# Attention's weighed sums of two steps stand together, with three buffers of probabilities and one of stacked operands; GpSimd in one loop over the routed tiles

## The reference, cut to what matters

```python
x = x + xattn(layernorm(x), ctx)      # 32 heads of 16; q and k are rms-normed per head
x = x + ffn(layernorm(x))             # one shared expert and 7 routed ones, top 2 of 7

def xattn(x, ctx):
    q, k, v = x @ Wq.T, ctx @ Wk.T, ctx @ Wv.T       # k and v interleaved by features
    scores = rmsnorm(q) @ rmsnorm(k).T * 16 ** -0.5
    return softmax(scores) @ v

def ffn(x):
    gate = x @ Wr + br
    _, ids = top_k(gate + gate_bias, 2)              # probs: softmax over the two chosen gates
    u = x @ Wup + bup                                # each expert
    g = silu(u @ Wgate + bgate) * u
    return sum_e(probs_e * (g @ Wdown + bdown)) + shared_expert(x)
```

## Time and profile before

| what | value |
|---|---|
| median of 3 runs | 972.75 us (972.32 to 972.9) |
| profiled execution | 973.43 us |
| its span (first to last instruction) | 971.7 us |
| mean granted clock of PE, share of full | 0.996 |
| busy: PE | 946.0 us (97%) |
| busy: PEld | 682.0 us (70%) |
| busy: DVE | 707.2 us (73%) |
| busy: ACT | 497.8 us (51%) |
| busy: POOL | 208.4 us (21%) |

### The profile page before, as it was taken

One profiled execution on the slowest core, in us unless ns is written; L12 is line 12 of the kernel. 1 busy time (PEld: TensorE's weight loads), 2 busy tenths in 40 slices (PEclk: granted clock), 3 DMA queues, 4 the chain that ended last, 5 costly groups with the idle time before them and its releaser, 6 DMA issues.

```text
span 971.7 us, 17895 instructions
## 1 busy us (share of the span) xinstructions
PE 946.0 (97%) x6676; PEld 682.0 (70%) x6676; DVE 707.2 (73%) x1459; ACT 497.8 (51%) x619; POOL 208.4 (21%) x226
## 2 busy tenths in 40 slices
PE   8999999999999999999999999899999999999995
PEld 6634444454434543446999889799999999999995
DVE  7798767886678767885978787665867686858654
ACT  4588668866787658887324223322424243424221
POOL 1011000311012200321300001333233333233331
PEclk9999999999999999999999999999999999999998
DMA  9400100101101110324413114633544536635533
GB/s 330 169 1 23 65 1 1 45 33 39 61 1 44 45 66 1 110 75 163 176 44 112 65 56 144 204 65 54 178 80 123 131 77 193 187 66 157 117 56 41
DMA packets 32512, 87.42 MB, mean 90 GB/s; under 512 B 7744, under 2 KB 7744, under 8 KB 28352
## 3 DMA queue, kind: packets, MB, share of 16 engines
q1 hardware_dynamic: 21920, 60.70, 17.8%
q0 software_dynamic: 10528, 25.87, 13.1%
HBM read 61.83 MB, written 24.72 MB: 89 GB/s over the span
## 4 chain that ended last, share of the span: by engine, by line
PE 83%; DVE 7%; DMA 4%; issue 3%; ACT 2%; POOLq 1%; DVEq 0%; POOL 0%; SPq 0%; ACTq 0%
PE z_ps L905 15%; PE y_ps L905 14%; PE u_ps L905 13%; PE o_ps L640 11%; PE scores L624 8%; PE bank_a L677 5%; PE bank_b L661 5%; PE bank_b L647 2%; PE xt_ps L917 2%; PE bank_a L647 2%; DMA out<-y_sb,target 2%; PE tr L706 1%; PE tr L700 1%; PE tr L695 1%; DMA xg<-xn_dram,index 1%
## 5 line engine op out<-in xcount | busy, mean ns | idle before, releaser
L1178 ACT ACTIVATE probs<-scores 128x2048 f32<-128x2048 f32 x128 | 240.7, 1880 | 64.1 <-PE scores L624 61.1
L905 PE MATMUL z_ps<-u_hi,w_sb 128*128 128x256 f32 x896 | 168.3, 285 | 0.7 <-DVE u_lo L1867 0.7
L905 PE MATMUL u_ps<-x_hi,w_sb 128*128 128x256 f32 x864 | 159.2, 282 | 0.0
L1208 ACT ACTIVATE u_hi<-u_ps,b_ug 128x256 fp32r<-128x256 f32 x108 | 45.4, 471 | 197.6 <-PE u_ps L905 176.3
L905 PEld LDWEIGHTS z_ps<-u_hi,w_sb 128*128 128x128 f32 x896 | 141.0, 190 | 2.1 <-DVE u_lo L1867 1.2
L905 PE MATMUL y_ps<-w_sb,g_hi 128*128 128x512 f32 x448 | 139.5, 392 | 0.2 <-DVE g_lo L1885 0.2
L905 PEld LDWEIGHTS u_ps<-x_hi,w_sb 128*128 128x128 f32 x864 | 135.7, 190 | 1.1
L640 PE MATMUL o_ps<-probs,v_sb 128*17 128x512 f32 x1024 | 134.7, 598 | 0.0
L905 PE MATMUL z_ps<-u_lo,w_sb 128*128 128x256 f32 x448 | 126.6, 282 | 0.0
L905 PE MATMUL u_ps<-x_lo,w_sb 128*128 128x256 f32 x432 | 122.0, 282 | 0.0
L1220 ACT ACTIVATE s_sb<-z_ps,b_ug 128x256 f32<-128x256 f32 x112 | 47.0, 472 | 103.4 <-PE z_ps L905 103.4
(11 more groups left out here) (248 smaller groups left out, 1596.3 us busy)
## 6 DMA issues: line engine op xcount, KB each, us to landing
w_raw<-w_all SPq DMA_DIRECT2D x27, 1024.0 KB, 7.7
ctx_raw<-ctx_t SPq DMA_DIRECT2D x4, 1024.0 KB, 6.8
out<-x_sb SPq DMA_DIRECT2D x16, 256.0 KB, 2.0
xg<-xt_dram POOLq DMA_DIRECT2D x14, 256.0 KB
x_sb<-x SPq DMA_DIRECT2D x1, 3072.0 KB, 17.2
xn<-x_t SPq DMA_DIRECT2D x12, 256.0 KB, 4.7
xn_dram<-xn SPq DMA_DIRECT2D x12, 256.0 KB, 2.1
xt_dram<-xt SPq DMA_DIRECT2D x6, 512.0 KB, 3.0
```

The lines of the kernel that those rows point to most:

```text
L905: ins = nc.tensor.matmul(out_ps, stat[a], mov[b], start=(first and a + b == 0), stop=(last and a == 1), skip_group_check=True)
L1178: nc.scalar.activation(probs[:, t % 2], scores[:], ACT.Exp).then_inc(p_ready, 1)
L1208: last = nc.scalar.activation(u_hi[:, c, :], u_ps[:, b, a, :], ACT.Identity, bias=b_ug[:, par, 0, c:c + 1])
```

## The change

In the attention: a step's `weighed` calls are given by a table, `SUMMED`, which says for each `s` which steps' sums stand in it. Pairs stand in steps 0, 3 and 6, single ones in 2 and 4, none in 1, 5 and 7. In steps 2 and 7 `between` comes ahead of them, in the others behind them. The turns are dealt out anew, few in the steps with a pair. The probabilities have three buffers, and ACT waits for `weighed(t-3)`. The stacked operands have one buffer; DVE waits in `half_scored` until the unit before has read its half. `sum_q` of step 7 comes ahead of the turns.

In the FFN: `table_part` moves from behind the up stage to behind the gate stage, and writes into `xt_ps`; `table_out` moves from ahead of `x_low` to the time of the down stage. GpSimd has a single loop, and waits for a scatter's landing at the start of the next scatter, behind the next gather.

```diff
-        probs = asb("probs", [P, 2, QUADS, SEQ])
+        probs = asb("probs", [P, 3, QUADS, SEQ])
...
-        q_st = asb("q_st", [P, 2, 2, SEQ], FP32R)
-        k_hi, k_lo = (asb(n, [P, 2, 2, CTX], FP32R) for n in ("k_hi", "k_lo"))
+        q_st = asb("q_st", [P, 2, SEQ], FP32R)
+        k_hi, k_lo = (asb(n, [P, 2, CTX], FP32R) for n in ("k_hi", "k_lo"))
...
-        K_TURNS = {6: (0, 4), 7: (4, 5), 0: (5, 9), 1: (9, 12)}
-        Q_TURNS = {3: (0, 5), 4: (5, 9), 5: (9, 12)}
+        K_TURNS = {6: (0, 1), 7: (1, 5), 0: (5, 6), 1: (6, 12)}
+        Q_TURNS = {3: (0, 1), 4: (1, 6), 5: (6, 12)}
+
+        SUMMED = {0: (-2, -1), 1: (), 2: (0,), 3: (1, 2), 4: (3,), 5: (), 6: (4, 5), 7: ()}
...
             def gather(n):
 
-                if isinstance(n, int):
+                first = isinstance(n, int) and n == NA
+                if first:
                     pool.wait_ge(xl_done, n * 2)
-                else:
-                    pool.wait_ge(xt_ready, (n - NT) * 2)
-                if isinstance(n, int):
                     pool.wait_ge(table_ready, 1)
                     pool.wait_ge(dense_stored, 16)
                 else:
+                    pool.wait_ge(xt_ready, (n - NT) * 2)
                     pool.wait_ge(row_saved, n - NA)
...
-            def scatter(n, more=True):
-
+
+            def scatter(n):
+                if not isinstance(n, int):
+                    pool.wait_ge(y_stored, (n - NA + 1) * 32)
+                    pool.sem_inc(passed)
...
-                if more:
-                    pool.wait_ge(y_stored, (n - NA + 2) * 32)
-                    pool.sem_inc(passed)
...
-            def turn(n, par, j):
-                gather(n + 1)
-                pool.wait_ge(out_stored, 16 * TILES)
-                scatter(n - 1)
-
-            total = routed(pool, lambda j, par, nth, first: None, turn)
-            scatter(total + NA - 1, more=False)
+
+            pool.wait_ge(start_ready, 1)
+            total = bound(pool, ER)
+            gather(NA + 1)
+            pool.wait_ge(out_stored, 16 * TILES)
+            scatter(NA - 1)
+            with pool.Fori(1, total) as i:
+                gather(i + (NA + 1))
+                scatter(i + (NA - 1))
+            scatter(total + (NA - 1))
...
                 elif s == 7:
                     if ahead:
+                        sum_q(u + 2)
                         k_turns(u + 2, *K_TURNS[s])
-                    if ahead:
-                        sum_q(u + 2)
...
             for u in range(UNITS):
                 for s in range(STEPS):
+
                     scored(u, s)
-                    between(u, s)
-                    if u or s:
-                        weighed(STEPS * u + s - 1)
+                    if s in (2, 7):
+                        between(u, s)
+                    for back in SUMMED[s]:
+                        if u or back >= 0:
+                            weighed(STEPS * u + back)
+                    if s not in (2, 7):
+                        between(u, s)
                     after(u, s)
             first_up(5 * UP_TURNS, len(UPS))
             pe.wait_ge(p_ready, STEPS * UNITS)
-            weighed(STEPS * UNITS - 1)
+            for t in (STEPS * UNITS - 2, STEPS * UNITS - 1):
+                weighed(t)
...
             def x_transposes(n):
                 if isinstance(n, int) and n < NT:
                     return
+                if isinstance(n, int):
+                    pe.wait_ge(window_read, 3)
...
-            def table_part(n, w):
+            def table_part(w):
 
                 pe.wait_ge(hots_ready, w + 1)
-                pe.wait_ge(y_done, 2 * n)
-                at = y_v[:, 0, 0:COLS]
+                pe.wait_ge(window_read, w + 1)
+                at = xt_ps[:, 0].rearrange("p a n -> p (a n)")[:, 0:COLS]
...
-            tile(5, 0, behind_up=lambda: table_part(5, 0), windows=2, bounds=range(1, DC + 1))
-            tile(6, 0, behind_up=lambda: table_part(6, 1), windows=3, bounds=range(DC + 1, ER + 1))
+            tile(5, 0, behind_z=lambda: table_part(0), bounds=range(1, DC + 1))
+            tile(6, 0, behind_z=lambda: table_part(1), bounds=range(DC + 1, ER + 1))
...
-                    if t > 1:
-                        act.wait_ge(pv_done, t - 1)
+                    if t > 2:
+                        act.wait_ge(pv_done, t - 2)
...
-                    nc.scalar.activation(probs[:, t % 2], scores[:], ACT.Exp).then_inc(p_ready, 1)
+                    nc.scalar.activation(probs[:, t % 3], scores[:], ACT.Exp).then_inc(p_ready, 1)
...
+            def half_scored(u, ab):
+                if u:
+                    dve.wait_ge(sc_ready, STEPS * (u - 1) + MT * (ab + 1))
...
-            tile(5, 0, x_tile=10, during_u=lambda: hot_cols(0), before_x=lambda: table_out(0),
-                 during_y=lambda: hot_rows(1))
+            tile(5, 0, x_tile=10, during_u=lambda: hot_cols(0),
+                 during_y=steps_of(lambda: table_out(0), lambda: hot_rows(1)))
...
-            tile(6, 0, x_tile=12, during_u=lambda: hot_cols(1), before_x=lambda: table_out(1),
-                 during_y=splits(1, 1, [1]))
+            tile(6, 0, x_tile=12, during_u=lambda: hot_cols(1),
+                 during_y=steps_of(lambda: table_out(1), splits(1, 1, [1])))
```

More of the change, by code:

```diff
@@ L623, in scored @@
                         rows = slice(32 * j, 32 * j + 32)
-                        last = nc.tensor.matmul(scores[:, j, :], part[rows, u % 2, ab, mt * P:(mt + 1) * P],
-                                                q_st[rows, u % 2, ab, :], start=(part is k_hi), stop=(part is k_lo),
+                        last = nc.tensor.matmul(scores[:, j, :], part[rows, ab, mt * P:(mt + 1) * P],
+                                                q_st[rows, ab, :], start=(part is k_hi), stop=(part is k_lo),
                                                 skip_group_check=True)
@@ L640, in weighed @@
                     last = nc.tensor.matmul(o_ps[32 * j:32 * j + HD + 1, :], v_sb[b % 2][:, mt, head, :],
-                                            probs[:, t % 2, j, :], start=(mt == 0), stop=(mt == MT - 1),
+                                            probs[:, t % 3, j, :], start=(mt == 0), stop=(mt == MT - 1),
                                             skip_group_check=True)
@@ L944, in table_part, with tile @@
                 last.then_inc(window_ready, 1)
-            def tile(n, par, j=0, behind_up=None, amid_z=None, behind_z=None, windows=0, bounds=()):
+            def tile(n, par, j=0, behind_up=None, amid_z=None, behind_z=None, bounds=()):
                 w = w_sb[par]
@@ L985, in tile @@
                     behind_z()
-                if windows:
-                    pe.wait_ge(window_read, windows)
-                elif known and n == 2:
+                if known and n == 2:
                     pe.wait_ge(gates_read, 1)
@@ L1425, in stack_q @@
                 done(nc.vector.stream_shuffle(twin[:], qn[:], (UPPER_TWICE, LOWER_TWICE)[ab]))
-                at = q_st[:, u % 2, ab, :]
+                at = q_st[:, ab, :]
+                half_scored(u, ab)
                 done(nc.vector.tensor_copy(at, twin[:]))
@@ L1433, in stack_k @@
                 done(nc.vector.stream_shuffle(twin[:], kn[:], (UPPER_TWICE, LOWER_TWICE)[ab]))
-                hi = k_hi[:, u % 2, ab, :]
+                hi = k_hi[:, ab, :]
+                half_scored(u, ab)
                 done(nc.vector.tensor_scalar(hi, twin[:], sign[:, 0:1], None, ALU.mult))
-                nc.vector.scalar_tensor_tensor(k_lo[:, u % 2, ab, :], twin[:], sign[:, 0:1], hi.bitcast(FP32),
+                nc.vector.scalar_tensor_tensor(k_lo[:, ab, :], twin[:], sign[:, 0:1], hi.bitcast(FP32),
                                                ALU.mult, ALU.subtract).then_inc(k_stacked, 1)
@@ L1845, in table_out @@
                 dve.wait_ge(window_ready, w + 2)
-                part = y_v[:, 0, 0:COLS]
+                part = xt_ps[:, 0].rearrange("p a n -> p (a n)")[:, 0:COLS]
                 if w == 0:
```

## The result

The changed kernel takes 966.92 us (median; 966.54 to 968.92). Its ratio to the kernel before is 0.9947 [0.9932, 0.9961]: faster by 0.53%, or 5.8 us, where 12.2 were forecast. Its profiled execution is one at the median, 966.92, with a span of 965.1.

What follows compares the result with a forecast made beforehand. PE, busy for 97% of the span at almost full clock, was taken as the bound. Attention -4.2 and FFN -8.0 make -12.2 us, from 972.75 to 960.5; range for 8 in 10: 956.5 to 966.5.

Steps and rivals of the forecast that it cites:

- Step 2: unchanged, 2.72: Attention, regular units: step 2 was to keep its length of 2.72 us.
- Steps 5 and 7 ... 2.72 each: Attention, regular units: PE work of 2.70 and 2.66 us, so 2.72 each by the exponential.
- The pair: Attention, steps 0, 3, 6: two adjacent weighed sums take 1.845 us, saving 0.115 a pair.
- a second sum saves nothing: Rival for the attention's pairs: weight loads don't overlap on the same rows; price 5.5 us, total 966.0; chance 0.12.
- Unit 0, -0.7: Attention, unit 0: three turns move from step 0 into step 1, where PE waits for the exponential; -0.7 us.
- Units 14 and 15, +2.6: Last two attention units: no turns to even out the pairs, so about 23.6 and 22.8 us; +2.6 us.
- The new waits, no cost: Attention: the third probabilities buffer and DVE's wait for the unit before cost nothing; tightest margin 2.3 us.
- The table, -2.1: FFN tiles 5 and 6: PE's stand of 1.05 us for DVE's one-hot columns goes; two tiles, -2.1 us.
- The first gather, "margin 1.8 us": FFN: index at 575.6, packets end at 581.3, transposes need them at 583.1; margin 1.8 us despite the later table.
- second rival: GpSimd part does less: tile 10's gather still late, or the first misses its 1.8 us; 962.5 to 966; chance 0.10.
- Tile 9's gather, -4.2, and the clock behind it, -1.35: FFN: PE's 4.15 us wait for gathered rows goes, -4.2; so does the clock's fall behind it, -1.35 us.
- The rival of the clock in units 14 and 15: Attention's last units: PE's clock falls in steps with little work, giving about 980 us; chance 0.04.

Runs made afterwards that it cites:

- e5: Changed kernel with step 1's output transposes between turns 9 and 10 instead of behind all six turns; 965.87 us.
- e6: Changed kernel, but from unit 14's step 1 on each step has one weighed sum, behind `between`, as before the change; 964.16 us.
- e8: Changed kernel with step 7's four turns ahead of `sum_q` instead of behind it; 973.72 us.
- e9: Changed kernel with the waits for the next unit's stacked operands ahead of step 7's last turn instead of the next scores; 966.19 us.
- e10: Changed kernel with `between` in the middle of pairs of weighed sums instead of behind them; 973.25 us.
- e4: Kernel before with only the new buffer counts and DVE's waits, turns and sums in the old order; 972.52 us.
- e7: Changed kernel with the table's matmuls in tiles 5 and 6 amid the gate stage and its reading ahead of `x_low`; 965.68 us.
- e2: Kernel before with only GpSimd's single loop, the wait for a scatter's landing behind the next gather; 967.37 us.
- e1: Kernel before with only the attention's part of the change; 973.28 us.
- e3: Kernel before with only `table_part` and `table_out` moved; 972.58 us.

## Why the prediction was wrong, point by point

The direction was right and the size was twice too large. Of the miss of 6.4 us, 4.75 is the attention and 1.3 the FFN; the start came 0.4 earlier by chance; and 0.7 is that I carried the offset of 0.68 of the profiled execution before over to after, whose profiled execution has none. In the attention, step 2 makes 2.8, step 7 1.4, unit 0 0.7 and the last two units 0.25; small differences elsewhere give 0.4 back.

- **"Step 2: unchanged, 2.72"** is the step that failed. Over units 0 to 13 step 2 is 2.8 us longer than forecast: 0.20 to 0.23 in each of the six regular units, 0.5 in unit 1, 0.3 to 0.36 in units 2, 6 and 10, nothing in the other four. I had summed PE's work, which fits into 2.72, and had not asked for the blocks of step 2 what they wait for once step 1 is longer and without a sum at its end. The weighed sum at the end of step 1 had given DVE and ACT the 1.0 us that they need between the transposes, or the last turn of k, and `sum_k`. e5 shows the first of the two dependences, and its timeline the second. In unit 1 the same wait for DVE at L704 is 0.44 long; it varies, for e6, which has the same order there, has 2.89 in place of 3.22. In units 2, 6 and 10 the wait for bank b (L651) makes 0.24 of it.
- **"Steps 5 and 7 ... 2.72 each"**: step 5 right, step 7 0.09 too short, 0.9 us in ten units, and 0.12 in the four units with gates. In the ten it is not the order (e8) but the two waits on the stacked operands (e9).
- **The pair**: right. 1.845 forecast, 1.84 measured; in e10 a cut pair costs 0.12 in its step. The 6.3 us that e10 loses come near the forecast's 5.5 in part by luck, since 1.7 of them are another wait. The rival "a second sum saves nothing" is refuted.
- **Unit 0, -0.7**: wrong. Step 0 is 0.69 shorter (6.65 to 5.96) and step 1 0.69 longer (2.97 to 3.66). ACT's exponential of step 1 starts 7.7 us behind the first scores in both kernels (33.14 to 40.84, 32.72 to 40.43), since it stands behind a logarithm in ACT's queue that waits for DVE's sum of squares. I took PE's hole there as room; it was the same limit, moved.
- **Units 14 and 15, +2.6**: right in the sum, +2.85, and step 3 takes 3.59 for a forecast 3.6. Unit 14 is 24.17 for a forecast 23.6, and the tail, which I had put at nothing, gives 0.3 back. e6 gives it all back.
- **The units with gates, -0.8**: right. Their step 7 gets 0.30 shorter, where the others' gets 0.13 shorter, so 0.17 of the forecast's 0.2 each.
- **The new waits, no cost**: right for the buffers and DVE (e4). Two small ones that I didn't name are there: `tr` at L704, and bank b at L651, 0.24 in step 2 of units 2, 6 and 10.
- **The table, -2.1**: the two stands are gone, as forecast: the table's matmuls follow the gate stage without a gap. From the end of the attention to the first routed transposes only 0.9 us are left of it, and e7 shows that the late gather had the rest.
- **The first gather, "margin 1.8 us"**: wrong, and the cause of that. Both its terms, 0.18 for the copy and 5.7 from index to the last packet, were measured at another place. Moved by 5 us, the copy took 0.7 longer, and the gather met the output's stores and a load of weights; 8.3 passed from index to landing. It was named as a possibility in the second rival.
- **Tile 9's gather, -4.2, and the clock behind it, -1.35**: right. Transposes, after:

```profile
620.94 1.04 PE L928 MATMUL xt_ps<-ident,xg 128*128 128x128 f32 x8
638.85 1.03 PE L928 MATMUL xt_ps<-ident,xg 128*128 128x128 f32 x8
```

  No wait, and 638.85 - 620.94 = 17.91 for the next tile, against 19.24. e2 shows no fall of the clock either, and has nearly the whole gain by itself.

- **The rival of the clock in units 14 and 15**: not in the profiled execution after. The profiled execution of e1 shows such a fall, in unit 15's step 0, behind the stand of 1.09 (a stretch, then PE's timeline):

```profile
430.00:432.00 2.00, 2.00 (x16) 0.37 (x16) 1.93 (x6) 1.34 (x1) 0.90 (x1) 0.54 0.12 44
```

```profile
429.74 0.50 PE L626 MATMUL scores<-q_st,k_hi 32*128 32x512 f32 x4 [1.09 <-ACT probs L1185]
...
430.56 3.39 PE L642 MATMUL o_ps<-probs,v_sb 128*17 128x512 f32 x16
```

  A granted clock of 0.54 is nearly all 1.2 GHz. The pair takes 3.39 instead of 1.91, and the step 1.6 us more. I had forecast all or nothing, 980 or no fall. Two executions of the changed kernel, 968.13 and 968.92, have a mean clock of 0.994 where the other three have 0.996 or 0.997; they may have had the same fall, but they have no trace. The same stand of 1.09 is in e5, e7 and e8, whose executions all have a mean clock of 0.996 or 0.997. So the stand doesn't bring the fall each time, and that it is the cause at all is argued from its place, not shown by a run.

One gain of the new loop I had not forecast: the times scatter less. In the kernel before, with its stand of 4 us in tile 9, the mean clock lies between 0.993 and 0.998, and its 28 executions beside e2's span 970.53 to 974.22. e2's six, without that stand, have 0.996 or 0.997 and span 967.0 to 967.84.

## What to carry to other kernels

When work is moved between the steps of a hand-written order, it is not enough to sum each step's work: for every block that stays, look up who reads its bank last and who makes its operand, and whether the piece that moved away had covered that. Holes of the bounding engine that are set by another engine's queue are no room for work moved into them. And a transfer's margin must be taken from a stretch with the traffic of its new place, not of its old one.

## What the runs showed of the hardware

- Two more semaphores directly ahead of the scores cost PE 0.09 us in units where both had been reached 2.2 us or more before (step 7 of 2.81). Ahead of the last turn they cost nothing (2.72, e9).
- Weight loads of a second weighed sum take place while the first one's matmuls run on the same rows (loads at 0.44 and 0.87 of a pair). Two such sums take 1.84, two single ones 1.96.
- The second indirect DMA of a gather landed 5.1 us after its issue among plain stores and a load of weights, at 0.93 of the DMA engines' time; in e7, where the first gather ran by itself, all four took 3.3 to 3.6.
- The same copy of 128 x 2 integers on GpSimd took 0.18 us where the last that it waited for was DVE's `x_lo` (before and e7), and 0.91 where it waited for the table itself (e3 and the changed kernel). Why is open.
- The granted clock fell to 0.54 over 2 us behind a stand of 1.09 us in one execution (e1), and not in the profiled executions of after, e5, e7 and e8 behind the same stand.
